# A bias added to the results of a small product instead of through a one-hot table

## The reference

```python
perm = (logits == jnp.max(logits, axis=-3, keepdims=True)).astype(x.dtype)
permuted = jnp.einsum('bntd,bntes->bnesd', grouped, perm)
inner = jax.nn.relu(jnp.einsum('bnesd,esdf->bnesf', permuted, W1) + b1)
result_permuted = jnp.einsum('bnesf,esdf->bnesd', inner, W2) + b2
result = jnp.einsum('bnesd,bntes->bntd', result_permuted, perm)
```

## Time and profile before

| | |
|---|---|
| Median of 3 runs | 2923.41 us (2923.05 to 2923.77) |
| The profiled execution | 2926.86 us, span 2925.1 us |
| PE matmul | 2769.8 us busy, 95% of the span |
| PE weight load | 2237.4 us, 76% |
| DVE | 2053.4 us, 70% |
| ACT | 1715.0 us, 59% |
| POOL | 1463.4 us, 50% |

### The profile page before, as it was taken

How to read it: one execution, slowest core, us unless ns; L and a number is a source line. 1 busy time by engine, 2 the same in 40 slices (tenths; PEclk the granted TensorE clock), 3 DMA queues, 4 the chain that set the end, 5 groups by cost and what they waited for, 6 DMA issues and landing times.

```text
span 2925.1 us, 135112 instructions
## 1 busy us (share of the span) xinstructions
PE 2769.8 (95%) x59836; PEld 2237.4 (76%) x59836; DVE 2053.4 (70%) x2871; ACT 1715.0 (59%) x3424; POOL 1463.4 (50%) x2319
## 2 busy tenths in 40 slices
PE   8999999999999999999999999999677787899998
PEld 7888888888888888888888888887566676455554
DVE  6777777777777777777777777777444443788998
ACT  5666566566666666656656656665333333666674
POOL 4666666666667667666666666666110000111111
PEclk9999999999999999999999999999899998899999
DMA  4222222222222222222222222222644443578776
GB/s 154 78 73 69 74 78 76 73 78 77 72 79 74 72 82 73 73 77 74 75 75 78 74 72 79 76 73 58 215 132 136 110 123 119 178 222 269 234 228 195
DMA packets 262711, 316.37 MB, mean 108 GB/s; under 512 B 28000, under 2 KB 184032, under 8 KB 260464
## 3 DMA queue, kind: packets, MB, share of 16 engines
q1 hardware_dynamic: 252176, 297.55, 33.7%
q10 hardware_dynamic: 9952, 10.17, 1.1%
HBM read 194.31 MB, written 113.31 MB: 105 GB/s over the span
## 4 chain that ended last, share of the span: by engine, by line
PE 89%; DVE 4%; issue 4%; DMA 1%; SPq 1%; POOL 1%; ACT 0%; ACTq 0%; DVEq 0%; POOLq 0%
PE a_proj L991 41%; PE a_mix L991 12%; PE s_ps L1714 6%; PE g_pick_ps L1465 6%; PE a_scan L1105 5%; PE s_ps L1735 4%; DVE g_picked L1394 3%; PE s_ps L1730 3%; PE a_scan L1082 3%; PE a_scan L1069 2%; PE g_acc_ps L1489 2%; PE a_mix L1057 2%; PE a_misc L1049 1%; PE a_misc L1123 1%; DMA part_dram<-res 1%
## 5 line engine op out<-in xcount | busy, mean ns | idle before, releaser
L991 PE MATMUL a_proj<-wdh,xTh 128*128 128x512 f32 x1024 | 421.2, 411 | 5.5 <-issue 3.7
L991 PE MATMUL a_proj<-wdh,xTl 128*128 128x512 f32 x1024 | 402.4, 393 | 0.3 <-issue 0.3
L991 PE MATMUL a_proj<-wdl,xTh 128*128 128x512 f32 x1024 | 400.0, 391 | 1.7 <-issue 1.7
L823 DVE COPY_PREDICATED scan_in<-mask,a_scan 64x512 f32<-64x512 uint32 x512 | 382.4, 747 | 16.1
L1671 ACT COPY s_stage<-s_ps 128x1024 f32<-128x1024 f32 x256 | 279.2, 1147 | 150.9 <-PE s_ps L1714 142.4
L464 POOL TENSOR_TENSOR dx<-xs,d_row 64x512 f32<-64x512 f32 x256 | 331.4, 1294 | 15.1
L472 POOL TENSOR_TENSOR yv<-yt,dx 128x512 f32<-128x512 f32 x128 | 189.0, 1476 | 293.2 <-DVE yt L863 293.2
L639 ACT ACTIVATE scan_in<-CT,hsel 64x128 f32<-64x128 f32 x1024 | 326.2, 388 | 4.8
L603 ACT ACTIVATE raw<-a_proj,rs 128x272 f32<-128x272 f32 x128 | 62.5, 488 | 427.4 <-PE a_proj L991 427.4
L1394 DVE COPY g_picked<-g_pick_ps 128x1024 f32<-128x1024 f32 x128 | 156.7, 1224 | 218.4 <-PE g_pick_ps L1465 218.4
L1691 DVE STREAM_TRANSPOSE s_turned<-s_stage 128x2048 f32<-128x2048 f32 x128 | 294.4, 2302 | 9.8 <-ACT s_stage L1671 9.8
(11 more groups left out here) (152 smaller groups left out, 7275.3 us busy)
## 6 DMA issues: line engine op xcount, KB each, us to landing
x<-in_x_dram SPq DMA_DIRECT2D x128, 256.0 KB, 2.7
xn_dram<-xn SPq DMA_DIRECT2D x128, 256.0 KB, 2.4
part_dram<-res SPq DMA_DIRECT2D x128, 256.0 KB, 2.5
g_xn<-xn_dram SPq DMA_DIRECT2D x512, 64.0 KB, 2.3
s_part<-part_dram SPq DMA_DIRECT2D x128, 256.0 KB, 4.1
out_dram<-s_out SPq DMA_DIRECT2D x128, 256.0 KB, 3.8
xr<-in_xT_dram SPq DMA_DIRECT2D x126, 256.0 KB, 2.9
s_inner<-inner_dram SPq DMA_DIRECT2D x32, 512.0 KB, 4.1
```

Of the source, the lines that this page charges most:

```text
L823: nc.vector.copy_predicated(dst, mask[rows_, :].unsqueeze(1).unsqueeze(1).to_broadcast([CH, 4, 2, CH]), src).then_inc(mt_cp, 1)
L991: last = nc.tensor.matmul(out, lhs[a], rhs[c], start=(k == 0 and n == 0), stop=(k == nk - 1 and n == 2))
```

## The change

The bias no longer goes through the one-hot table. It is written into the four banks of a unit ahead of the W2 products, which then accumulate on it. Four matmuls do that, one for each bank, each in a row tile of its own. Each contracts 8 rows: four experts times high and low part. Its stationary operand `spread` sends a row to the 32 output rows of its expert.

For this the bias is laid out differently (`b2`, [128, 8, 512], 32 rows used), and split into high and low part by POOL at the start of block 2 of the gather stage (`split_b2`), in eight pieces of [128, 512]. SP loads each piece with four transfers of 16 KB in every second step of block 2 (`load_b2`), after POOL has finished the piece before; ahead of the first stand the loading of `spread` and a wait for POOL's memsets. The rounding on ACT and DVE goes, as does the wait for it. `perm` is plain fp32.

```diff
@@ sync_program of the gather stage
                     load_xn(sync, e // 4 + 4, e % 4, i)
+            if b == 2 and w % 2 == 0:
+                scatter["load_b2"](sync, w // 2)
@@ gpsimd_program of the gather stage
         for b in range(NGB):
+            if b == 2:
+                scatter["split_b2"](pool)
             for i in range(2):
                 pool.wait_ge(acc_cp, 2 * b + i + 1)
@@ scalar_program, vector_program of the gather stage
-        scatter["round_b2"](act)
-        scatter["rest_b2"](dve)
@@ scatter_phase
+    def load_b2(sync, x):
+        if x == 0:
+            sync.wait_ge(zeroed, 2)
+            sync.dma_start(spread_raw[:], io["spread"]).then_inc(b2_in, 16)
+        else:
+            sync.wait_ge(b2_ready, x + 1)
+        for r in range(4):
+            rows_ = slice(ES * r, ES * r + 8)
+            sync.dma_start(b2_raw[rows_, :], io["b2"][8 * r:8 * r + 8, x, :]).then_inc(b2_in, 16)
+
+    def split_b2(pool):
+        for i in range(2):
+            pool.wait_ge(att["res_out"][i], 16 * NST)
+        nc.gpsimd.memset(ones[:], 1.0).then_inc(zeroed, 1)
+        nc.gpsimd.memset(b2_raw[:], 0.0).then_inc(zeroed, 1)
+        pool.wait_ge(zeroed, 2)
+        for x in range(NH * QB):
+            pool.wait_ge(b2_in, 16 * (4 * x + 5))
+            if x == 0:
+                nc.gpsimd.tensor_tensor(spread[:], spread_raw[:, 0:P], ones[:].to_broadcast([P, P]), ALU.mult).then_inc(b2_ready, 1)
+            wait(pool, b2_ready, x + 1)
+            nc.gpsimd.tensor_tensor(b2_high[:], b2_raw[:], ones[:].to_broadcast([P, 2 * DH]), ALU.mult).then_inc(b2_high_ready, 1)
+            pool.wait_ge(b2_high_ready, 2 * x + 1)
+            nc.gpsimd.tensor_tensor(b2_high[:].bitcast(F32), b2_high[:].bitcast(F32),
+                                    spread_raw[:, P:P + 1].to_broadcast([P, 2 * DH]), ALU.mult).then_inc(b2_high_ready, 1)
+            pool.wait_ge(b2_high_ready, 2 * x + 2)
+            nc.gpsimd.tensor_tensor(b2[:, x, :], b2_raw[:], b2_high[:].bitcast(F32), ALU.add).then_inc(b2_ready, 1)
@@ apply_w2
         wait(pe, w2_cp, 2 * u if u < 4 else 2 * u - 1)
+        if u == 0:
+            pe.wait_ge(b2_ready, NH * QB + 1)
+        for r in range(4):
+            rows_ = slice(ES * r, ES * r + 8)
+            nc.tensor.matmul(bank[:, pair(u, r // 2), :, :][:, r % 2, :, :], spread[rows_, :], b2[rows_, k * QB + i, :],
+                             start=True, stop=False, skip_group_check=True)
...
                     last = nc.tensor.matmul(dst, inner[m % NINNER][rows_, 8 * c + 2 * i + j, :], w2[rows_, i, 2 * c + j, :],
-                                            start=True, stop=True)
+                                            start=False, stop=True, skip_group_check=True)
@@ gather_results
-            for t in range(2):
-                tile = slice((2 * x + t) * P, (2 * x + t + 1) * P)
-                for n in range(2):
-                    nc.tensor.matmul(dst[:, t, :], perm[m % 2][:, tile], b2[n][:, cols], start=(t == 0 and n == 0), stop=False,
-                                     skip_group_check=True)
...
-                                            turned[m % 2][:, g * (SG // GPT // 2) + x, :, t], start=False, stop=True,
+                                            turned[m % 2][:, g * (SG // GPT // 2) + x, :, t], start=(t == 0), stop=True,
```

More of the change, by code:

```diff
@@ L70 @@
 AT_W1, AT_PERM0, AT_XNT, AT_ONEHOT, AT_XN3, AT_PICKED, AT_INNER, AT_PERM1, AT_SMALL, AT_TOP, AT_END = (
-    0, 65536, 70144, 86528, 102912, 119296, 184832, 201216, 205312, 206336, 212832)
+    0, 65536, 70144, 86528, 102912, 119296, 184832, 201216, 205312, 206336, 228192)
 def placer(nc, prefix, start, stop):
@@ L1368, in negate_b1, with gpsimd_program @@
         nc.gpsimd.tensor_scalar(b1neg[:], b1[:], -1.0, 1.0, ALU.mult, ALU.mult).then_inc(b1_ready, 1)
-    def gpsimd_program(pool):
+    def gpsimd_program(pool, scatter):
         for b in range(NGB):
+            if b == 2:
+                scatter["split_b2"](pool)
             for i in range(2):
@@ L1542, in scatter_phase @@
     inner = [sb(f"inner{i}", [P, NQ, SG], at=a) for i, a in enumerate((AT_PERM1, AT_PERM0, AT_XN3 + 12288))]
-    perm = [sb(f"perm{i}", [P, CT], F32R, at=AT_XN3 + 4096 * i) for i in range(2)]
+    perm = [sb(f"perm{i}", [P, CT], at=AT_XN3 + 4096 * i) for i in range(2)]
     permT = [sb(f"permT{i}", [P, CT], BF16, at=AT_XN3 + 8192 + 2048 * i) for i in range(2)]
-    b2 = [sb(f"b2{n}", [EX, D], F32R, at=AT_TOP + 2048 * i) for i, n in enumerate("hl")]
-    b2_raw = sb("b2_raw", [EX, D], at=AT_TOP + 4096)
-    ones = sb("ones", [P, 1], at=AT_TOP + 6144)
+    b2 = sb("b2", [P, NH * QB, 2 * DH], F32R, at=AT_TOP + 5376)
+    b2_high = sb("b2_high", [P, 2 * DH], F32R, at=AT_TOP)
+    b2_raw = sb("b2_raw", [P, 2 * DH], at=AT_TOP + 2048)
+    spread_raw = sb("spread_raw", [P, P + 1], at=AT_TOP + 4096)
+    spread = sb("spread", [P, P], F32R, at=AT_TOP + 4640)
+    ones = sb("ones", [P, 1], at=AT_TOP + 5152)
     part = [sb(f"part{i}", [P, 2, DH]) for i in range(NPART)]
@@ L1556, in scatter_phase @@
     zeroed = sem("zeroed")
-    b2_hi = sem("b2_hi")
-    b2_lo = sem("b2_lo")
+    b2_high_ready = sem("b2_high_ready")
+    b2_ready = sem("b2_ready")
     perm_ready = sem("perm_ready")
@@ L1646, in spread_perm @@
             nc.gpsimd.tensor_tensor(perm[m % 2][:], permT[m % 2][:], ones[:].to_broadcast([P, CT]), ALU.mult).then_inc(perm_ready, 1)
-        pool.wait_ge(att["res_cp"], 2 * NST)
-        nc.gpsimd.memset(ones[:], 1.0).then_inc(zeroed, 1)
-        pool.wait_ge(zeroed, 1)
         for m in range(STEPS):
             spread_perm(m)
[L1654 to L1662, removed]
     def evict(act, u):
@@ L1720, in gather_results @@
             m, x = divmod(v, QB)
-            cols = slice(m // NSET * DH, (m // NSET + 1) * DH)
             if x == 0:
@@ L1727, in gather_results @@
             for t in range(2):
-                tile = slice((2 * x + t) * P, (2 * x + t + 1) * P)
-                for n in range(2):
-                    nc.tensor.matmul(dst[:, t, :], perm[m % 2][:, tile], b2[n][:, cols], start=(t == 0 and n == 0), stop=False,
-                                     skip_group_check=True)
-            for t in range(2):
                 for g in range(GPT):
                     tok = (2 * x + t) * P + GRP * g
-                    last = nc.tensor.matmul(dst[GRP * g:GRP * g + GRP, t, :], perm[m % 2][:, tok:tok + GRP].bitcast(F32),
-                                            turned[m % 2][:, g * (SG // GPT // 2) + x, :, t], start=False, stop=True,
+                    last = nc.tensor.matmul(dst[GRP * g:GRP * g + GRP, t, :], perm[m % 2][:, tok:tok + GRP],
+                                            turned[m % 2][:, g * (SG // GPT // 2) + x, :, t], start=(t == 0), stop=True,
                                             skip_group_check=True)
             last.then_inc(out_ps, 1)
-        pe.wait_ge(b2_lo, 1)
         for u in range(4, UNITS + LAG):
@@ L1747, in scatter_phase @@
     return dict(sync=sync_program, gpsimd=gpsimd_program, scalar=scalar_program, vector=vector_program, tensor=tensor_program,
-                load_first=load_first, apply_w2=apply_w2, evict=evict, round_b2=round_b2, rest_b2=rest_b2)
+                load_first=load_first, apply_w2=apply_w2, evict=evict, load_b2=load_b2, split_b2=split_b2)
 def program(nc, io):
@@ L1774, in _ @@
                 att["gpsimd"](pool, gat)
-                gat["gpsimd"](pool)
+                gat["gpsimd"](pool, sca)
                 sca["gpsimd"](pool)
@@ L1829, in layout @@
         w2=L0_ffn_W2.reshape(4, 4, 2, 4, NH, DH, ES).transpose(4, 1, 3, 6, 0, 2, 5).reshape(NH, 4, P, 8, DH),
-        b2=L0_ffn_b2.reshape(EX, D),
+        b2=np.broadcast_to(L0_ffn_b2.reshape(4, 4, 2, 4, NH, DH).transpose(3, 0, 4, 1, 2, 5)[:, :, None],
+                           (4, 4, 2, NH, 4, 2, DH)).reshape(32, NH * 4, 2 * DH),
+        spread=np.stack([np.append(np.arange(P) // GRP == k % ES // 2, -(k % 2)) * (k % ES < 8) for k in range(P)]).astype(np.float32),
         ident=np.eye(P, dtype=np.float32),
@@ L1843 @@
     from concourse.bass_utils import run_bass_kernel_spmd
-    nc = bacc.Bacc("TRN2", target_bir_lowering=False, num_devices=1)
+    nc = bacc.Bacc("TRN2", target_bir_lowering=False, num_devices=1, dynamic_dma_scratch_size=1024)
     arrays, io = {}, {}
```

1 line of the change is left out of this document (removed).

## The result

The changed kernel took 2942.38 us as a median of 4 runs, the kernel before 2923.59 us, now with a fourth run. The ratio is 1.0059, with a 95% interval from 1.0046 to 1.0072: the change costs about 17 us (18.8 by the two medians), more than a measurement of this kernel leaves open. A second set of runs gave 1.0055 (1.0036 to 1.0074).

What follows compares the result with a forecast made beforehand. PE looked like the bound, DVE close behind; after the change, a ring of ACT and PE. Steady loop 8.3 + before unit 9 5.4 - tail 2.6 + split 10 = +21.1 us, 2945 us; 8-in-10 range 2928 to 2962.

Steps and rivals of the forecast that it cites:

- The total: Whole kernel: +21.1 us on the 2923.41 us median, given as 2945 us; chance 0.62, own range 2936 to 2960.
- The ring of ACT and PE: Steady scatter units: bias waits for ACT's first copy, PE idles 0.23 us, period 3.20 us, +8.3 us over 118 periods.
- The bias stage: Four new bias matmuls per scatter unit, running together: 0.50 us with drain, 0.42 without, replacing 0.67 us of PE.
- The 13.7 us of scattered waits: Scatter units 9 to 127: missing instructions and a late DMA, 0.116 us a period above 3.133, left as they are.
- Before unit 9: First scatter units, 0 to 9: new bias of 0.50 to 0.8 us enters each of units 0 to 8; together +5.4 us.
- The tail: Last four gathers lose their bias stages of about 3.3 us, 0.7 given back at the low clock; net -2.6 us.
- The split: Gather stage, block 2: POOL's chain delays its additions, ACT's store and the copy behind it by 10.5 us; +10 us.
- The rule on row tiles: Bias matmuls: speedup 3.07 would make columns cost 0.28 instead of 0.21 us, steady loop another 8 us longer; not adopted.
- The hidden split: Gather stage: split pieces under 5.7 us, through faster 16 KB transfers or shorter POOL operations; 2935 us, chance 0.16.
- Matmuls one behind the other: Scatter units: four bias matmuls run in a row, bias 1.1 us, period 3.80; 3020 us, chance 0.09.
- The case with nothing to see: Whole kernel: bias at 0.42 us and the split hidden; 2925 us, chance 0.07.
- The faster case: Scatter units: copy done when the gather ends, PE saves 0.16 us a unit; 2918 us, chance 0.06.

Runs made afterwards that it cites:

- The two experiments: Split spread over blocks 2 and 3 in the changed kernel: 2926.96 us, 1.0033 of before; loads and unused split added to the kernel before: 1.0022.

## Why the prediction held, point by point

**The total** was right: 2945 us forecast, 2942 measured, and slower; as a change, +21 forecast, 17 to 19 measured. Its parts were less right than the total, and that they add up as well as they do is partly luck.

**The ring of ACT and PE** was right as a mechanism. The bias starts 1.26 us after the W2 share ends (1.27 forecast), PE idles 0.22 (0.23), and the row names ACT. Removing the bias shortened a unit by 0.40, doubling it lengthened it by 0.23, and starting the copy earlier shortened it by 0.13.

**The bias stage** was mis-sized: 0.50 forecast, 0.43 measured, near my lower bound of 0.42 without a drain. The forecast put 0.12 to 0.15 us for a drain between the bias and W2, a length that no row shows by itself. PEld idles there only 0.24 to 0.25, where it idles 0.41 to 0.43 between the other groups. So the period was not 3.20 but 3.11 to 3.13, with one in four at 3.21. That one is the first unit of a set: the bias starts 1.31 to 1.33 us after the W2 share there, and PEld's idle row names its own issue instead of ACT; PE's list has one wait more there, for the set's inner results; that this wait is the reason was not tested. The regular units cost +1.8 us, not +8.3.

**The 13.7 us of scattered waits**, which the prediction left as they are, did not stay: 14.8 on average became 21.8, +7 us. This error and the one before it cancel by luck, and the stage came out 8.9 us longer where 8.3 was forecast. What makes late units more frequent is not settled. They are half as long with less traffic, in one pair of profiles. Fuller DMA engines go with them in most profiles, but not in all. The length of the unit does not order them: 39.5 us at 2.75 us a unit and 22.8 and 23.1 at 3.00, but 25.3 at 3.20 and 14.5 at 3.36 with the bias twice, as little as in the kernel before although its bias stands in the ring. None of these separates the changed kernel from the one before, whose units are equally long and whose traffic is the same; and the pair with less traffic kept a gap of 16 us with late sums only 3 apart.

**Before unit 9**: +5.4 forecast, +4.0 measured. That it is the bias is shown by the kernel without it, where this stretch takes 37.6 us as in the kernel before. The bias is shorter at the low clock too (0.73 from 2504.29 to 2505.02, where 0.8 was forecast); over nine units that is 0.6 of the missing 1.4, and the rest is open. These two rows of weight loads have the stage at the low clock:

```profile
2504.29 0.29 PEld L1734 LDWEIGHTS s_ps<-s_b,s_spread 8*128 8x128 f32 x4 [2.03 <-ACT s_stage L1692]
2505.02 0.28 PEld L1741 LDWEIGHTS s_ps<-s_w,s_inner 32*32 32x32 f32 x32 [0.44 <-issue]
```

**The tail**: -2.6 forecast, -1.7 measured. The four last gathers now follow each other without a gap, as said, and take 5.66 us:

```profile
2929.21 5.66 PE L1756 MATMUL s_ps<-s_turned,s_perm 128*32 128x256 f32 x64 [3.12 <-DVE s_turned L1712]
```

against 8.36 before (2913.35 to 2921.71); the stretch from gather 119 to the end still gains only 2.0 in that profile and 1.7 on average, so 0.7 to 1.0 us is given back around them.

**The split** was right in every link: the chain began at 2188.64, ended 55.6 us later (59.1 forecast, a piece 6.7 us instead of 7.2), and held ACT's store and the copy behind it. +10 forecast, +7.9 measured. The chain is 3.5 us shorter than forecast, which is more than the difference of 2.1; the return at the low clock was there. The two experiments give 6.4 and 7.6, so this term was somewhat too large.

**The rule on row tiles.** The Trainium skill, "TensorE: Matmul & The Clock Gate", section "Measured speedup vs the span model", gives four row tiles 3.07 times the speed of one. Here four matmuls of 512 columns add 0.23 us to a unit, where one alone would need 0.213 at one column per cycle, or 0.24 at the pace of the old bias matmuls. By this trace the factor is between 3.7 and the full 4. By the Trainium skill's figure the stage would, as an estimate, be longer by some 8 us; the measurement decides against it here.

**The rivals.** The hidden split (2935 us) fell with the 10.31 us of ACT. Matmuls one behind the other (3020) fell with the doubled bias. The case with nothing to see (2925) had its bias right, 0.43 for 0.42, but not its split. The faster case (2918) would have needed a copy under 0.88 us; it takes 1.09. A shorter way to the same gain, an earlier copy, reached 3.00 us a unit and no further.

## What to carry to other kernels

Work that is moved behind a wait for another engine can cost its full length even where it makes its own engine less busy: add up the ring that closes through the wait (copy, moved work, products), not the engine. An operation of an engine with slack can still hold another one by what stands behind it in its list, so a chain of small loads and splits should leave the regular work its due times; here two blocks instead of one gave back 6.4 us. And scattered waits are a term of the sum: when the steady part is known to a hundredth of a microsecond, they are what can move.

## What the runs showed of the hardware that was not expected

- Sixteen tiles of 32x32 take 64 matmuls of 256 fp32 columns in 1.42 us. With eight tiles for the second half of them it is 1.42 as well, with eight tiles throughout 1.73.
- PEld's idle time between the 8*128 bias loads and the 32*32 loads behind them is 0.24 to 0.25 us; between 32*32 and 128*32, and between 128*32 and 8*128 without a wait for ACT, it is 0.41 to 0.43. It holds columns that still stream, too: with the bias twice it is 0.37 in the first place.
- PE stops with nothing to wait for 8 to 14 times between 2521 and 2880 us, up to 2.3 us at a time and 7.8 to 13.5 us in all (seven profiles with the stage of before or of the change). With the stage's traffic down from 223 to 152 GB/s it is 6 stops and 5.0 us in the changed kernel, and 5 stops and 2.4 us in the kernel before (one profile each).
- On POOL, the last operation of the split (128x512, fp32 in, fp32r out) takes 1.26 us and the two before it, one of them with fp32r out as well, 1.04.
